# Three PSUM banks for the second scores of a cross-attention, one for the preparations

## The reference, cut to what matters

```python
q = _split_heads(query @ Wq.T)
k = _split_heads(key @ Wk.T)
v = _split_heads(value @ Wv.T)
scores = jnp.einsum('bhqd,bhkd->bhqk', q, k) * inv_scale
scores = jnp.where(mask[:, None, :, :] == 0, min_val, scores)
attn = jax.nn.softmax(scores.astype(jnp.float32), axis=-1).astype(scores.dtype)
ctx = jnp.einsum('bhqk,bhkd->bhqd', attn, v)
return ctx.transpose(0, 2, 1, 3).reshape(query.shape[0], -1, D) @ Wo.T
```

## Time and profile before

| | us |
|---|---|
| median of 3 runs (2555.08 to 2559.41) | 2556.68 |
| the profiled execution: its time | 2558.81 |
| its span, first to last instruction | 2556.8 |
| its mean granted TensorE clock | 0.801 |

### The profile page before, as it was taken

One profiled execution on the slowest core, in us unless ns is written; L12 is line 12 of the kernel. 1 busy time (PEld: TensorE's weight loads), 2 busy tenths in 40 slices (PEclk: granted clock), 3 DMA queues, 4 the chain that ended last, 5 costly groups with the idle time before them and its releaser, 6 DMA issues. The chain is left out here.

```text
span 2556.8 us, 37341 instructions
## 1 busy us (share of the span) xinstructions
PE 1810.9 (71%) x12012; PEld 1047.7 (41%) x12076; DVE 1589.8 (62%) x6659; ACT 961.8 (38%) x1796; POOL 264.1 (10%) x239
## 2 busy tenths in 40 slices
PE   6999830394727888852596950699999999814875
PEld 3776520142625555442264640334343343313553
DVE  4479999898657888731010112767767777266984
ACT  1355432352004666620110200256666666512331
POOL 2000000000000000004000022000000000034652
PEclk8555555697868999975798985699999999956997
DMA  3011110234010000002505016222222220010000
GB/s 118 28 59 55 60 59 26 65 130 154 2 63 9 2 10 10 2 17 102 177 17 181 25 47 138 55 55 42 35 62 42 42 42 1 1 34 1 1 0 33
DMA packets 92069, 127.89 MB, mean 50 GB/s; under 512 B 11624, under 2 KB 69410, under 8 KB 90750
## 3 DMA queue, kind: packets, MB, share of 16 engines
q1 hardware_dynamic: 74196, 95.99, 13.6%
q10 hardware_dynamic: 14640, 22.28, 2.5%
q0 software_dynamic: 3072, 7.53, 1.0%
HBM read 85.41 MB, written 41.24 MB: 50 GB/s over the span
## 5 line engine op out<-in xcount | busy, mean ns | idle before, releaser
L1195 DVE CUSTOM_DVE_ANT_0 xam_junk<-xam_s,xa_mask_q 128x512 bf16<-128x512 f32 x512 | 339.6, 690 | 151.0 <-PE xam_s L1100 150.0
L1268 ACT ACTIVATE xam_exp<-xam_s 128x512 f32<-128x512 f32 x512 | 301.4, 598 | 184.9 <-PE xam_s L1134 129.6
L1100 PE MATMUL xam_s<-xa_kT,xa_qT 96*128 96x512 bf16 x512 | 201.5, 396 | 16.5 <-DVE xam_max L1195 13.1
L1131 PE MATMUL xam_s<-xa_qT,xa_kT 99*128 99x512 bf16 x512 | 196.7, 384 | 9.1 <-ACT xam_exp L1268 8.9
L1134 PE MATMUL xam_s<-xa_mask_k,identb 128*128 128x512 bf16 x452 | 172.2, 381 | 0.0
L353 PE MATMUL ps_d<-xnT,ctxT 128*32 128x112 f32 (+4 forms) x3168 | 158.0, 348 | 10.0 <-ACT stage L497 8.8
L430 DVE TENSOR_TENSOR_SCAN cost<-m,cost,dist_chunk 128x33 f32<-128x33 f32 x576 | 164.2, 285 | 0.2 <-issue 0.2
L1195 DVE CUSTOM_DVE_ANT_0 l0m_junk<-l0m_s,l_tri_q 128x128 bf16<-128x128 f32 (+3 forms) x256 | 118.7, 488 | 43.0 <-PE l0m_s L1100 40.3
L359 PE MATMUL ps_d<-rows_j,share 4*128 4x112 f32 (+4 forms) x396 | 140.6, 456 | 0.8 <-ACT rows_j L469 0.8
L1717 PE MATMUL ex_up<-ex_xT,ex_w 128*128 128x512 f32 x256 | 121.3, 634 | 25.6 <-DVE ex_xT L1749 13.4
L1147 PE MATMUL xam_o<-xam_exp,xa_vt 128*32 128x512 f32 x1024 | 137.2, 605 | 0.0
(11 more groups left out here) (329 smaller groups left out, 3601.7 us busy)
## 6 DMA issues: line engine op xcount, KB each, us to landing
xa_kT<-keys_d SPq DMA_DIRECT2D x96, 128.0 KB, 4.6
dist_chunk<-dist SPq DMA_DIRECT2D x36, 264.0 KB
values_d<-kv_values SPq DMA_DIRECT2D x16, 512.0 KB, 2.7
ex_w<-L_ffn_W ACTq DMA_DIRECT2D x8, 1024.0 KB, 18.8
ex_w<-L_ffn_W SPq DMA_DIRECT2D x8, 1024.0 KB, 16.2
xa_mask<-mask_BxSxS_ik SPq DMA_DIRECT2D x4, 2048.0 KB, 11.6
xa_vt<-values_d SPq DMA_DIRECT2D x16, 512.0 KB, 6.6
keys_d<-kv_keys SPq DMA_DIRECT2D x16, 384.0 KB, 2.5
```

The source lines that it names most:

```text
L1100: nc.tensor.matmul(ps1[n % 2][:, 0:w], qT[0:STK, slot(g, h), qt * P:(qt + 1) * P], kT[0:STK, slot(g, h), f * 512:f * 512 + w], start=True, ...
L1131: nc.tensor.matmul(o[:, q0:512], kT[:, slot(g, h), kt * P:(kt + 1) * P], qT[:, slot(g, h), q0:512], start=True, stop=False)
L1195: nc.vector.tensor_tensor_reduce(junk[:, n % NJ, 0:w], ps1[n % 2][:, 0:w], heads.bias_q(g, qt, f), 1.0, NEG * 4, ALU.add, ALU.max, mx[:, g ...
L1268: nc.scalar.activation(ebuf[at % NE][:, q0:512], ps2[at % 2][:, q0:512], ACT.Exp).then_inc(exped, 1)
```

## The change

`attend` gets `NS = 4 - heads.preps` banks for the second scores, and the preparations get `heads.preps` banks. The self-attention has `preps = 2`, and nothing changes there. The cross-attention has `preps = 1`: three banks for the second scores and one for the preparations. All waits are written for the new numbers; no work is added, removed or reordered.

```diff
-        self.bank = [nm.ps(f"prep{i}", [P, 512]) for i in range(2)]
+        self.bank = [nm.ps(f"prep{i}", [P, 512]) for i in range(self.preps)]
...
-            if rn >= 2:
-
-                for who in self.takers(self.rounds[rn - 2][2]):
-                    pe.wait_ge(self.freed[who], self.taken(who, rn - 2))
-            bank = self.bank[rn % 2]
+            if rn >= self.preps:
+
+                for who in self.takers(self.rounds[rn - self.preps][2]):
+                    pe.wait_ge(self.freed[who], self.taken(who, rn - self.preps))
+            bank = self.bank[rn % self.preps]
...
-        ps2 = [nm.ps(f"s2_{i}", [P, 512]) for i in range(2)]
+        NS = 4 - heads.preps
+        ps2 = [nm.ps(f"s2_{i}", [P, 512]) for i in range(NS)]
...
-                    if n >= 2:
-
-                        pe.wait_ge(exped, n - 1)
+                    if n >= NS:
+
+                        pe.wait_ge(exped, n - NS + 1)
                     q0 = kt * P if causal else 0
-                    o = ps2[n % 2]
+                    o = ps2[n % NS]
...
-                        nc.scalar.activation(ebuf[at % NE][:, q0:512], ps2[at % 2][:, q0:512],
+                        nc.scalar.activation(ebuf[at % NE][:, q0:512], ps2[at % NS][:, q0:512],
...
 class SelfHeads(Heads):
+    preps = 2
...
 class CrossHeads(Heads):
+    preps = 1
```

## The result

The changed kernel takes 2559.77 us (median of 20 runs) against 2555.44 us for the one before (20 runs, beside it): ratio 1.002, 95% interval 1.0012 to 1.0028. That is 3 to 7 us more, 4.3 between the medians; 4.8 had been forecast. The small difference is the rest of two larger ones.

A forecast was written before the change was run, and what follows sets the result against it. TensorE was taken to set the pace in the cross-attention. Gain −11.1, turn 1 +12.7 and +2.2 +1.0 ahead of the first step give +4.8 us on 2556.7: 2561.5 us, range 2557 to 2570.5 with the late-start rival.

The forecast's parts named there:

- The third bank's gain: Cross-attention second scores no longer wait for a late exponential: 8.1 + 0.5 + 2.5 = 11.1 us less.
- 14 starts of a step: Steps 2 to 15: the opening second score loses its wait, 8 × 0.55 + 6 × 0.62 = 8.1 us less.
- the last step: Sixteenth step: six waits of 0.41 us behind exponential pairs vanish, 2.5 us less; 0.5 more at its start.
- The rival in which `keep_max` keeps the start late: Step starts: `keep_max`, not the exponential, releases the first second score, 8.6 us stay, 2570.1 us; 8 in 100.
- The pause at turn 1: Unit 8 of 14 steps: turn 1 waits for VectorE's copy of turn 0, 14 × 0.91 = 12.7 us more.
- The hand-over: From the end of turn 0's copy to turn 1: 0.05 us to the load, 0.02 more to its matmul.
- Ahead of the first step: Four mask rounds wait for the single bank, 2.2 us more; second step's turn 1, 1.0 us more.
- The sum: Whole kernel: −11.1 + 12.7 + 2.2 + 1.0 = +4.8 us, forecast 2561.5 us.
- The clock: Rival, in the steps: new pauses drop TensorE's clock to 1.2 GHz for a few us, 28 us, 2590 us; 4 in 100.

The follow-up runs named there:

- the square of four: Regular steps: kernel before 35.83 us, changed kernel 36.14, changed kernel with only two second-score banks 36.76, changed kernel with turn 1 at unit 10 35.21.
- the first profile: Changed kernel's profile: first projection to first second score 49.4 us, against 44.3 before; a second profile of it, unchanged, took 46.2 there, 2559.11 us whole.

## Why the prediction held

**The third bank's gain**, forecast 11.1 us: 0.55 or 0.62 at 14 starts of a step, as forecast (8.1); 2.66 in the last step against 2.5; and 0.70 at its start, where the idle time was 0.83 and the second score now starts 0.06 behind `keep_max`. The last was put at 0.5. Some 11.5 in all. The rival in which `keep_max` keeps the start late falls at the 14 starts: there the second score follows the first score by 0.22. Only at the sixteenth does `keep_max` now hold it, by about 0.3. And the run with one preparation and two score banks has the waits back.

**The pause at turn 1**, forecast 14 × 0.91 = 12.7 us: the square of four gives 0.93, so 13.0. The hand-over from the copy to load and matmul was 0.06; the prediction had 0.05 from the mask round and 0.02 more as an estimate that no row shows. TensorE stood still for 0.90, and the next second score follows turn 1 another 0.03 later than before.

**Ahead of the first step**, forecast 2.2 + 1.0 = 3.2 us: measured 5.1 in the first profile and 1.9 in the second. This is the term that was mis-sized, and in two ways that work against each other. At the high clock it is smaller than forecast: the second step's projection starts 1.6 later after the first one than before (17.4 against 15.8), where 2.2 was forecast, and what follows took 0.3 longer, where 1.0 was forecast. And the clock, which was set to 0 and kept for the range, added 1.6 in the projection alone in one execution and nothing in the other.

**The sum**: −11.5 + 13.0 + 5.1 = 6.6 with the first profile's clock, −11.5 + 13.0 + 1.9 = 3.4 with the second's. The runs say 3 to 7. The two large terms were forecast to some 0.4 us each; that the sum of 4.8 lies as near as 0.5 to the medians' 4.3 is in part luck, for the stretch ahead of the first step differs by 3 us between two executions.

**The clock** did not fall in the steps: from 1700 to 2150 us it stayed at 1.00 (third figure from the end) with the pauses in it, as in the earlier trace rows.

```profile
1700.00:2150.00 450.00, 435.41 (x2756) 181.13 (x2752) 318.84 (x1007) 292.55 (x489) 8.55 (x13) 1.00 0.24 45
```

An edit that gives one group a third bank and takes another group's second was worth the difference of two waits here, 0.62 and 0.93 in a regular step, and both could be read from the trace before the edit was made.

## What to carry to other kernels

Price a buffer from both ends: list which matmul, not which weight load, waited for the reader, and for the group that loses a buffer, the distance between a round and its neighbour against the time in which the neighbour is read out. If one neighbour is too close, move it before taking the buffer: here two units of distance turned a loss of 5 us into a gain of 4, with no buffer more. And ask which of the groups has the costlier waits, and in which stage: in the steps the bank gave a little more at the second scores, ahead of them 4.5 us more at the first scores, by one profile of each.

## What the runs showed that was not expected

The granted clock ahead of the first step differs between executions of one program. The second step's projection took 3.51 us in one execution of the changed kernel and 1.90 in another, with the clock at 0.50 and 0.87 in the same 14 us. A single profile of a stretch in which TensorE is only partly busy is a sample of one. The steps, from the second on at a clock of 1.00, repeat to 0.02 us. And the time up to the first projection, in code that the change and the experiments leave alone, ran from 1611.3 to 1617.3 us over the ten profiles; so the whole time of one execution can't price a change of 5 us, and the steps can.
